# A gated attention layer on one core: swapped base rows written by ScalarE, and small transfers issued ahead of later loads

## The reference, cut to what matters

```python
mu = jnp.mean(x, axis=-1, keepdims=True)
var = jnp.mean(jnp.square(x - mu), axis=-1, keepdims=True)
xn = (x - mu) / jnp.sqrt(var + EPS) * ln_w + ln_b
uv = jax.nn.silu(xn @ uv_w.T + uv_b)
u, v, base = (uv[..., :E], uv[..., E:2 * E], uv[..., 2 * E:])     # E = 512, S = 128 columns of base
base = base[:, :, None, :] * gamma[None, None] + beta
base = _rope(base)                        # x1*cos - x2*sin, x2*cos + x1*sin over the two halves
q, k = (base[:, :, 0, :], base[:, :, 1, :])
qk = jnp.einsum('bis,bjs->bij', q, k)
kernel = jnp.square(jax.nn.relu(qk / SQRT_S + bias[None]))
out = u * jnp.einsum('bij,bje->bie', kernel, v)
return out @ o_w.T + o_b + shortcut
```

## Time and profile before

| | us |
|---|---|
| median of 3 runs | 2699.27 |
| lowest and highest of them | 2690.11, 2700.03 |
| profiled execution, first to last instruction (span) | 2695.2 |
| last layer in it, from its first transfers at 1957.3 to the end | 737.9 |

### The profile page before, as it was taken

One profiled execution on the slowest core, in us unless ns is written; L12 is line 12 of the kernel. 1 busy time (PEld: TensorE's weight loads), 2 busy tenths in 40 slices (PEclk: granted clock), 3 DMA queues, 4 the chain that ended last, 5 costly groups with the idle time before them and its releaser, 6 DMA issues. The chain is left out here.

```text
span 2695.2 us, 57058 instructions
## 1 busy us (share of the span) xinstructions
PE 2580.1 (96%) x20386; PEld 2360.3 (88%) x20386; DVE 2038.1 (76%) x6162; ACT 1513.0 (56%) x3098; POOL 1013.1 (38%) x905
## 2 busy tenths in 40 slices
PE   7999999979999999999999999999959999899997
PEld 6999999968999999999899999999847887778886
DVE  6899998858888888888888888888557556755554
ACT  4788887746676675666667566676435212541111
POOL 3232232234424424344352433424035434533342
PEclk8999999979999999999999999999969999999999
DMA  2011221122222222223322222222332112221111
GB/s 81 20 35 40 91 66 51 34 74 89 70 84 76 89 76 73 88 92 102 100 86 80 72 91 70 85 80 66 95 130 79 51 39 82 78 80 32 32 32 40
DMA packets 223614, 190.59 MB, mean 71 GB/s; under 512 B 22372, under 2 KB 205800, under 8 KB 222312
## 3 DMA queue, kind: packets, MB, share of 16 engines
q1 hardware_dynamic: 204616, 177.30, 20.8%
q10 hardware_dynamic: 18720, 9.64, 1.3%
HBM read 91.13 MB, written 44.04 MB: 50 GB/s over the span
## 5 line engine op out<-in xcount | busy, mean ns | idle before, releaser
L1272 POOL TENSOR_TENSOR b_sb_r_norm<-b_sb_squares,b_sb_power 128x8 f32<-128x8 f32 x64 | 105.1, 1642 | 667.6 <-DVE b_sb_squares L1440 667.6
L1362 ACT ACTIVATE b_sb_probs<-b_sb_probs,b_sb_neg_top,b_sb_r_norm 128x256 f32<-128x256 f32 x512 | 262.6, 590 | 47.1 <-DVE b_sb_neg_top L1490 46.3
L2138 ACT ACTIVATE c_kern_hi<-c_kern 128x512 fp32r<-128x512 f32 x128 | 81.0, 632 | 364.9 <-DVE c_kern L2260 364.9
L2041 POOL TENSOR_TENSOR c_kern_lo<-c_kern,c_kern_hi 128x512 fp32r<-128x512 f32 x128 | 172.0, 1345 | 292.0 <-ACT c_kern_hi L2138 292.0
L39 PE MATMUL psum<-b_sb_fT_lo,b_sb_w_hi 128*128 128x256 f32 x768 | 219.8, 286 | 1.4 <-DVE b_sb_fT_lo L1548 1.4
L40 PE MATMUL psum<-b_sb_fT_hi,b_sb_w_lo 128*128 128x256 f32 x768 | 216.5, 282 | 0.0
L41 PE MATMUL psum<-b_sb_fT_hi,b_sb_w_hi 128*128 128x256 f32 x768 | 216.5, 282 | 0.0
L1483 DVE CUSTOM_DVE_ANT_0 b_sb_probs<-psum,b_sb_mask 128x256 f32<-128x256 f32 x512 | 195.3, 419 | 17.9 <-PE psum L1653 17.5
L39 PE MATMUL psum<-c_kern_lo,c_v_hi 128*128 128x512 f32 x512 | 204.3, 399 | 0.0
L41 PE MATMUL psum<-c_kern_hi,c_v_hi 128*128 128x512 f32 x512 | 200.5, 392 | 0.0
L40 PE MATMUL psum<-c_kern_hi,c_v_lo 128*128 128x512 f32 x512 | 200.5, 392 | 0.0
(11 more groups left out here) (308 smaller groups left out, 8826.8 us busy)
## 6 DMA issues: line engine op xcount, KB each, us to landing
b_sb_v_prev<-b_sb_v_now SPq DMA_DIRECT2D x64, 260.0 KB, 2.3
b_sb_kT_hi<-b_sb_kT_hi SPq DMA_DIRECT2D x64, 256.0 KB, 2.7
b_sb_kT_lo<-b_sb_kT_lo SPq DMA_DIRECT2D x64, 256.0 KB, 3.0
Y<-b_sb_y SPq DMA_DIRECT2D x128, 128.0 KB, 2.2
b_sb_res<-Y SPq DMA_DIRECT2D x64, 128.0 KB, 2.1
b_sb_x_f<-Y SPq DMA_DIRECT2D x128, 64.0 KB, 2.3
b_sb_res_f<-Y SPq DMA_DIRECT2D x64, 128.0 KB, 2.3
U<-c_u_out SPq DMA_DIRECT2D x16, 512.0 KB, 4.4
```

Of the source, the lines that this page charges most:

```text
L1272: pool.tensor_tensor(r, s, p, ALU.pow).then_inc(r_ready[1][b], 1)
L1362: ins = act.activation(probs[b][:, n, :], probs[b][:, n, :], ACT.Exp, bias=neg_top[b][:, n:n + 1], scale=r_norm[b][:, h:h + 1])
L2041: pool.tensor_tensor(kern_lo[i % RING][:], kern[i % RING][:], kern_hi[i % RING][:].bitcast(F32), ALU.subtract)\
L2138: act.activation(kern_hi[i % RING][:], kern[i % RING][:], ACT.Copy).then_inc(hi_ready, 1)
```

## The change

Only the last layer changes, in four places. The swapped base columns leave the weights (C_PROJ is 1152 instead of 1280) and the matmuls; base has 6 matmuls in a step. ScalarE reads the one result three times: once straight, and once for each half of 64 partitions, written 64 partitions up or down. The bias sums have 10 columns' matmuls instead of 12 and b_col 5 columns instead of 6. On VectorE the second half of weights() becomes shifts() and comes behind hT_lo of step 0. On SyncE a slot's order is rope table, U store, residual, and then the load of the step four ahead. The region rows of C_EARLY grows by what w_raw loses, so that the addresses behind it stay.

```diff
-C_PROJ = 2 * C_E + 2 * C_S
+C_PROJ = 2 * C_E + C_S
+HALF = C_S // 2
...
-C_EARLY = {"ident": (P,), "w_raw": (KC, C_PROJ), "b_v_raw": (C_E,), "d_w": (KC, D), "rows": (2 * D,), ...}
+C_EARLY = {"ident": (P,), "w_raw": (KC, C_PROJ), "b_v_raw": (C_E,), "d_w": (KC, D), "rows": (2 * D + KC * C_S,), ...}
...
             for slot in range(first_slot, last_slot):
+                for n in step_in(slot):
+                    next_rope(n)
+                    u(n)
+                for n in step_in(slot + 1):
+                    residual(n)
                 for n in step_in(slot + 4):
                     load(n)
-                for n in step_in(slot + 1):
-                    residual(n)
-                for n in step_in(slot):
-                    u(n)
-                    next_rope(n)
...
                 ring.wait_full(act, ("base", n))
-                for k in range(2):
-                    ins = act.activation(base[:, k, :], ring.out(("base", n), 512)[:, k * C_STEP:(k + 1) * C_STEP], ACT.Silu,
-                                         bias=b_col[:, C_EC + k:C_EC + k + 1])
+                act.activation(base[:, 0, :], ring.out(("base", n), C_STEP), ACT.Silu, bias=b_col[:, C_EC:C_EC + 1])
+                for to, of in ((slice(0, HALF), slice(HALF, C_S)), (slice(HALF, C_S), slice(0, HALF))):
+                    ins = act.activation(base[to, 1, :], ring.out(("base", n), C_STEP)[of, :], ACT.Silu, bias=b_col[of, C_EC:C_EC + 1])
...
                                              in1=w_hi[:, c, :].bitcast(F32), op0=ALU.mult, op1=ALU.subtract).then_inc(w_ready, 1)
+
+            def shifts():
                 dve.wait_ge(row_in, 80)
...
                 for n in step_in(slot + 1):
                     turn_h(n)
+                    if n == 0:
+                        shifts()
...
-                for n, col in enumerate(list(range(0, C_E, P)) + [2 * C_E, 2 * C_E + P]):
+                for n, col in enumerate(list(range(0, C_E, P)) + [2 * C_E]):
...
                 ring.wait_bank(pe, ("base", n))
-                for k in range(2):
-                    ins = columns(n, ("base", n), k, 2 * C_E + k * P)
-                ring.written(ins, ("base", n))
+                ring.written(columns(n, ("base", n), 0, 2 * C_E), ("base", n))
...
-        "c_w": rows(np.concatenate([uv_w, swapped(uv_w[:, 2 * C_E:])], 1)),
-        "c_b_col": cols(np.concatenate([uv_b[:C_E], uv_b[2 * C_E:], swapped(uv_b[2 * C_E:])])),
+        "c_w": rows(uv_w),
+        "c_b_col": cols(np.concatenate([uv_b[:C_E], uv_b[2 * C_E:]])),
```

More of the change, by code:

```diff
@@ L1768 @@
 C_TILES = BATCH * C_CHUNKS * NT
-C_EARLY = {"ident": (P,), "w_raw": (KC, C_PROJ), "b_v_raw": (C_E,), "d_w": (KC, D), "rows": (2 * D,), "x_in": (2, D), "y_in": (2, D), "gb": (2, KC)}
+C_EARLY = {"ident": (P,), "w_raw": (KC, C_PROJ), "b_v_raw": (C_E,), "d_w": (KC, D), "rows": (2 * D + KC * C_S,), "x_in": (2, D), "y_in": (2, D), "gb": (2, KC)}
 C_LINE = 2 * SEQ
@@ L1863, in layer_c @@
         o_b, wo = sb("o_b", [P, D]), sb("wo", [P, C_EC, D])
-        gamma, beta, b_col = sb("gamma", [P, 2, 2]), sb("beta", [P, 2, 2]), sb("b_col", [P, C_EC + 2])
+        gamma, beta, b_col = sb("gamma", [P, 2, 2]), sb("beta", [P, 2, 2]), sb("b_col", [P, C_EC + 1])
         w_sign, d_bias, alpha = sb("w_sign", [P, KC, D], F32R), sb("d_bias", [P, D]), sb("alpha", [P, 1])
@@ L1891, in layer_c @@
         ones, total, delta = over("ones", kern_at, [P, P]), over("total", kern_at + 512, [P, 1]), over("delta", kern_at + 544, [P, 2])
-        b_raw = over("b_raw", kern_at + 608, [P, C_EC + 2])
+        b_raw = over("b_raw", kern_at + 608, [P, C_EC + 1])
         ring = Slots(sem, psum, "c_ring", list(bank_uses()))
@@ L2203, in weights @@
                 ring.wait_full(dve, ("shifts", 1))
-                ring.read(dve.tensor_tensor(b_col[:], ring.out(("shifts", 0), C_EC + 2), b_raw[:], ALU.add), ("shifts", 0))
+                ring.read(dve.tensor_tensor(b_col[:], ring.out(("shifts", 0), C_EC + 1), b_raw[:], ALU.add), ("shifts", 0))
                 ring.read(dve.tensor_tensor(b_v_raw[:], ring.out(("shifts", 1), C_E), b_v_raw[:], ALU.add), ("shifts", 1))
@@ L2349, in shifts @@
                 ring.wait_bank(pe, ("shifts", 0))
-                for n, col in enumerate(list(range(0, C_E, P)) + [2 * C_E, 2 * C_E + P]):
+                for n, col in enumerate(list(range(0, C_E, P)) + [2 * C_E]):
                     for c in range(KC):
-                        ins = pe.matmul(ring.out(("shifts", 0), C_EC + 2)[:, n:n + 1], w_raw[:, c, col:col + P], gb[:, 1, c:c + 1],
+                        ins = pe.matmul(ring.out(("shifts", 0), C_EC + 1)[:, n:n + 1], w_raw[:, c, col:col + P], gb[:, 1, c:c + 1],
                                         start=(c == 0), stop=(c == KC - 1))
```

## The result

The changed kernel takes 2681.53 us (median of 4 runs, 2677.64 to 2686.76) beside 2699.65 of before (4 runs, 2690.11 to 2700.43): a ratio of 0.994, 95% interval 0.9921 to 0.996. The total agrees better than its terms do, as the rest shows.

A forecast was written before the change was run, and what follows sets the result against it. TensorE, busy 96% of the span, was taken as the bound, so only fewer matmul columns or its waits count. Start 4.7, rope table 5.8, clock 0.8 and base rows 5.8 make 17.1 us: 2682.2 forecast, range 2672 to 2691.

The forecast's parts named there:

- The start: Step 0 of the last layer: fewer bias sums and shifts() behind hT_lo gain 4.7 us, ends 3.2 and 5.8.
- The delay beside GpSimd: Step 0: shifts() on VectorE runs beside GpSimd's residual; about 1.3 us lost once gives 4.5, twice 3.2.
- The rope wait: Step 1: SyncE's new order removes VectorE's whole 5.76 us wait for the rope table, gaining 5.8, ends 4.5 and 5.8.
- Rival 1: Step 1: the rope table lands no sooner, queued behind bias and x loads; 5.8 lost, 2688.0 us; chance 0.14.
- The clock: TensorE behind the 9.13 us wait of step 1: less time at half clock, 0.8 us gained, ends 0 and 1.7.
- The steady steps: Base rows on ScalarE: 0.30 us in each of ten waiting steps, 0.70 in four others; 5.8, ends 3.8 and 9.8.
- half as much again: ScalarE's two half activations: the upper bound on their added cost, 0.6 us a step, where 0.4 was taken.
- list of signs: What would show the forecast wrong: halves not costing about 0.4 us, GpSimd waiting for x, rope table over 8 us, clock 0.50 behind steady waits.
- four steps without moments: Steps 6, 7, 14 and 15, where VectorE has no moments: the whole 0.70 us counts in each, 2.8 together.
- Its cover: Steps 6, 7, 14, 15: 24 u matmuls (2.8 us), values matmuls and VectorE's missing moments hide the longer ScalarE chain.
- Rival 2: Steady steps: six waits grown from 0.95 to 1.35 drop the clock, costing 8.1 us together, 2690.3 us; chance 0.09.
- Rival 3: ScalarE: writing partitions 0 to 63 from 64 to 127 is dear; at 2.4 us added per step 2714 us; chance 0.05.

The follow-up runs named there:

- e2: The kernel before with only the four bias instructions moved behind hT_lo on VectorE; 2691.6 us in one profiled run, last layer 731.34 us.
- e8: The changed kernel with unread matmuls filling TensorE's waits ahead of the transposes of step 2 and the scores of tile 0; last layer 719.92 us.
- e1: The kernel before with only SyncE's new order; 2690.69 us in one profiled run, last layer 729.38 us.
- e6: The kernel before with a slot's second kern tile put ahead of the rope product and the moments on VectorE; 2677.74 us, ratio 0.9938 to before.
- e5: The changed kernel with a slot's second kern tile put ahead of the rope product and the moments on VectorE; 2654.42 us, ratio 0.9843 to before.
- e3: The kernel before with only ScalarE writing the swapped base rows; 2691.38 us in one profiled run, last layer 733.36 us.
- e7: The changed kernel with ScalarE's two half activations in the other order; last layer 723.29 us, first activation to scaling 1.48 us.
- e4: The changed kernel with swapped base rows written in four forms by step; first activation to scaling 0.88 (two wholes), 1.48 (crossed halves), 1.34 (uncrossed), 1.25 us (three wholes).
- e9: The kernel of e5 with the unread matmuls of e8 added; 2653.2 us, ratio 0.9837 to before, last layer 690.81 us.

## Why the prediction was right, and where its terms were not

**The start, predicted 4.7 (3.2 to 5.8), measured 5.9.** The rope product of step 0 starts at t0 + 21.35 instead of t0 + 27.28, and e2 alone gives 5.88. The delay beside GpSimd that was taken off did occur (the working gives 4.5 for one such delay; 4.7 was taken): the last bias subtraction took 1.70 us where an undisturbed one takes 0.68, with a GpSimd sum of 1.30 from 1978.18 on. The lock that was cited from the Trainium skill ("SBUF — State Buffer", SBUF: two separate sides) agrees with this row. But it fell on a piece of VectorE that had 1.41 us to spare, the wait ahead of the rope product above, so it cost nothing. The step that failed was to put the delay on the path. The upper end was a little low as well: the table load did not wait for the cast of b_rows, which ended at 1978.29; it began at 1977.97, as base ended. Only the activation behind the load needs the cast: in e8, where base ended 0.9 earlier, it waited 0.43 for it.

**The rope wait, predicted 5.8, measured 5.7 to 5.9.** VectorE has no wait for the table and ScalarE none for U; e1 alone gives 5.73. What is late next is the norm, as forecast: ahead of the scores of tile 0 TensorE waits 2.82, where 3.4 was expected, and ahead of the transposes of step 2 the 1.88 that it waited before became 2.57. Rival 1, the table that lands no sooner, falls: it landed in 2.9 us in the median, and VectorE found it there 8.3 us behind its issue.

**The clock, predicted 0.8 (0 to 1.7), measured 0 and worth 2.7.** From the scores of tile 0 to the transposes of step 3 after takes 20.17 us and before 20.37, and the 0.20 is the 0.10 of two steps. (The row that the prediction cites for a nearly full clock, shows busy time only; the mean granted clock of the span of before is 0.972.) The prediction took the half clock as the price of one long wait. But waits of 2.57 and 2.82 dropped it too: 0.50 from 1996 to 2002, then again from 2006 to 2012 behind 3.10. The fillers of e8 show what a held clock gives in the first of these stretches, 2.7 us, more than the upper end.

**The steady steps, predicted 5.8 (3.8 to 9.8), measured about 3.** This is the term that was mis-sized. Six matmuls less are 0.70, the added activation is 0.60, and the 0.10 that is left is what the steps from 1 to 5 show. TensorE's wait ahead of the transposes goes from 0.94 to 1.53, where 1.35 was expected. The bound "half as much again" was right, 0.4 wasn't: the prediction took over the pace of two whole activations (0.84 us for both, the second 0.37 behind the first), and the crossed halves begin 0.49 behind one another. By its own list of signs this one, half activations that don't cost about 0.4, counts against it. The Trainium skill's 93 ns of overlap ("ScalarE: Activation LUTs", What ACT_TABLE_LOAD costs) agrees with whole activations behind one another (0.47 long, 0.38 apart) and not with these halves (0.49 apart). In the four steps without moments 0.70 was expected each, 0.45 came in step 6: the transposes of step 7 begin 0.93 us behind the start of the last values product, where before it was 0.68. VectorE's kern and TensorE in after:

```profile
2079.11 0.69 DVE L2259 SCALAR_TENSOR_TENSOR c_kern<-psum,c_bias 128x512 f32<-128x512 f32 x1
...
2079.47 0.39 PE L41 MATMUL psum<-c_kern_hi,c_v_hi 128*128 128x512 f32 x1
2079.95 0.63 PE L2376 MATMUL psum<-c_ident,c_xn 128*128 128x128 f32 x4
```

Here 0.48 lies between the last matmul's start and the transposes', against 0.23 in before. Kern ends at 2079.80 and the transposes start 0.15 later, as they do behind the waits of 1.53; in before they start 0.50 behind kern. So 0.25 of the 0.70 became a new wait for kern. Its cover, the u and values matmuls, was named in the prediction; it was just not long enough for 0.60. What took the rest in steps 7 and 14 (0.33 and 0.49) wasn't followed up; between e6 and e5 both gain 0.7.

In steps 8 to 13 the 0.79 is a sum of three steps with 0 to 0.10 and three jumps, -0.47, -0.31 and 1.37. They lie behind the three long waits, where the half clock lasted 4.1, 4.2 and 5.9 us in before, and 5.1, 5.1 and 3.3 in after. The sum belongs to the base rows: e3 and e7, which have them, gain 0.80 and 0.78 in these steps with the same three lengths, e1 and e2, which haven't, -0.29 and 0.32. Why the lengths differ stays open.

**Rival 2**, steady waits that drop the clock, falls for the waits of 1.53: the clock is 1.00 from 2044 to 2094. In the steady steps it is 0.50 only behind the longest waits for kern (5.0 before, 5.6 after), in both kernels. **Rival 3**, a dear crossing, falls: 0.47 for a half.

**The sum.** 17.1 forecast for a layer that gained 14.8: +1.2 at the start, 0 at the rope table, -0.8 for the clock, -2.8 in the steady steps, which leaves 0.1 to rounding. The medians of the runs differ by 18.1, and the ratio's interval reaches from 10.8 to 21.3 us, so it holds both. That the median of 2681.5 lies within 1 us of the 2682.2 forecast is in part luck: of the 18.1 us the last layer shows 14.8, and the steady steps, one of the two largest terms, were forecast at twice what they brought.

## What to carry to other kernels

Moving a step ahead of a queue that it doesn't depend on paid twice here: 5.7 us for a wait of 5.76, which the timeline had priced, and 5.9 for a wait of 4.17, to which the overlap of matmuls and the clock added. Taking matmuls off TensorE where it waits for another engine gave 0.1 of 0.7 us a step, since the work went to the engines it waits for; with that wait moved out of the way first, the same change was worth 23.4 us instead of 14.8, 0.9 of it by the clock at the start. When work goes to an engine in more pieces, look at the distance between the starts, not only at their durations.

## What the runs showed of the hardware

- A ScalarE activation of 64x256 takes 0.47 us, as one of 128x256, and reading partitions 64 up or down doesn't lengthen it. Of these activations, which read one PSUM tile, the next begins 0.37 to 0.38 us after the start when both keep the first partition that they read and write, and 0.47 to 0.49 when either changes (e4, e7).
- Waits of 2.57 and 2.82 us one after the other left the granted clock at 0.50 for some 6 us of matmuls in after; the same block behind matmuls that nobody reads ran at 1.00, 7.46 us instead of 10.18 with the wait in it. In e1 the clock came back 3.4 us after the block's start. What decides between 3.4 and 6 no run here tells.
- The same instructions can meet either clock: base of step 0 ran at half clock in after, e4, e7 and e9 (0.41 us for a matmul of 128x256) and at full clock in e5 and e8 (0.28), and ScalarE's first step behind it began 0.96 us later or earlier by that (e9, e5).
- The rope table of 256 KB landed in 2.9 us (median) when it was issued ahead of the U store and the x loads, in 4.6 behind them. SyncE's order alone does it: 2.8 in e1, 4.6 in e2 and e3.
